# A transformer layer on eight cores: the layer norm's last step moves from VectorE to ScalarE, and the feed-forward norm is written three tiles ahead

## The reference

```python
def _layernorm(x, axis=-1, eps=1e-5):
    m = jnp.mean(x, axis=axis, keepdims=True)
    v = jnp.var(x, axis=axis, keepdims=True)
    return (x - m) / jnp.sqrt(v + eps)

x = x + attention(_layernorm(x))      # 16 heads of 128, causal, ALiBi bias, Wq Wk Wv Wo
x = x + ffn(_layernorm(x))            # below

def ffn(x):
    base = x @ W.T + b
    logits = x @ gate_w.T + gate_b
    topk_logits, topk_idx = top_k(logits, 2)
    gates = softmax(topk_logits)
    xA = einsum('nd,erd->ner', x, lora_A)
    delta = einsum('ner,eor->neo', xA, lora_B)
    return base + sum of the two chosen experts' delta * gates
```

## Time and profile before

| | us |
|---|---|
| times of two runs | 4712.88 and 4902.75 (median 4807.81) |
| the profiled execution | 4714.45, span 4712.9 on its slowest core |
| spans of the eight cores in it | 4694.5 to 4712.9 |
| PE busy | 3643.4 (77% of the span) |
| DVE busy | 1916.0 (41%) |
| ACT busy | 1149.2 (24%) |

### The profile page before, as it was taken

How to read it: one execution, slowest core, us unless ns; L and a number is a source line. 1 busy time by engine, 2 the same in 40 slices (tenths; PEclk the granted TensorE clock), 3 DMA queues, 4 the chain that set the end, 5 groups by cost and what they waited for, 6 DMA issues and landing times. The chain is left out here.

```text
span 4712.9 us, 65585 instructions; the slowest of 8 cores (4694.5 to 4712.9 us)
## 1 busy us (share of the span) xinstructions
PE 3643.4 (77%) x18452; PEld 1719.2 (36%) x18452; DVE 1916.0 (41%) x5424; ACT 1149.2 (24%) x2606; POOL 111.1 (2%) x210
## 2 busy tenths in 40 slices
PE   3588888988987694877735888888888876948777
PEld 1233434434434242333312334344344332413333
DVE  3435445455455121333334354554554551113333
ACT  3323333233233100011143232332332331000111
POOL 0000000000000001000000000000000000010000
PEclk8687787888878896888856878888888788968888
DMA  3211110110110646111131111101101106561111
GB/s 115 59 19 23 19 23 15 19 23 15 23 19 11 159 161 134 63 63 72 63 121 50 23 19 19 23 15 23 19 15 23 19 18 153 163 132 63 63 72 63
DMA packets 55537, 258.38 MB, mean 55 GB/s; under 512 B 13720, under 2 KB 13984, under 8 KB 34720
## 3 DMA queue, kind: packets, MB, share of 16 engines
q0 software_dynamic: 36464, 119.66, 13.0%
q1 hardware_dynamic: 11824, 84.20, 5.6%
q10 hardware_dynamic: 6912, 50.33, 3.0%
HBM read 273.15 MB, written 67.11 MB: 72 GB/s over the span
## 5 line engine op out<-in xcount | busy, mean ns | idle before, releaser
L852 ACT ACTIVATE prT<-dg,cstt 128x128 bf16<-128x128 f32 (+1 forms) x576 | 216.4, 386 | 1808.4 <-DVE dg L824 1328.9
L813 DVE TENSOR_SCALAR sp<-ps 128x512 f32<-128x512 f32 (+3 forms) x1104 | 631.6, 593 | 13.7 <-PE ps L806 5.4
L806 PE MATMUL ps<-QT,KT 128*128 128x512 bf16 (+3 forms) x1104 | 494.0, 489 | 184.4 <-DVE sp L813 143.6
L1118 PE MATMUL cb<-wf,cT 128*128 128x512 bf16 x2048 | 528.0, 421 | 95.3 <-DMA wf<-wf 83.6
L877 ACT ACTIVATE prT<-sp,cstt 128x128 bf16<-128x128 f32 (+2 forms) x1368 | 578.9, 488 | 16.8 <-DVE sp L813 9.8
L420 PE MATMUL bp<-wo,zTt 128*128 128x512 bf16 x2048 | 469.9, 393 | 97.1 <-DMA wo<-wo 74.1
L633 PE MATMUL pp<-xnT,wv 128*128 128x512 bf16 x2048 | 474.5, 394 | 0.0
L633 PE MATMUL pp<-xnT,wq 128*128 128x512 bf16 x2048 | 456.2, 384 | 0.0
L633 PE MATMUL pp<-xnT,wk 128*128 128x512 bf16 x2048 | 451.6, 381 | 0.0
L744 PE MATMUL pz<-va,prT 128*128 128x129 bf16 x3652 | 393.2, 266 | 26.5 <-ACT prT L877 11.4
L1118 PEld LDWEIGHTS cb<-wf,cT 128*128 128x128 bf16 x2048 | 214.6, 107 | 390.5 <-issue 205.7
(11 more groups left out here) (105 smaller groups left out, 2369.4 us busy)
## 6 DMA issues: line engine op xcount, KB each, us to landing
bx<-x SPq DMA_DIRECT2D x32, 1024.0 KB, 6.5
x2d<-b POOLq DMA_DIRECT2D x32, 1024.0 KB, 8.4
c<-x2d ACTq DMA_DIRECT2D x32, 1024.0 KB, 4.8
out<-co SPq DMA_DIRECT2D x32, 1024.0 KB, 3.9
prT<-x ACTq DMA_DIRECT2D x16, 1024.0 KB, 5.7
prT<-x SPq DMA_DIRECT2D x16, 1024.0 KB, 5.9
wv<-wv POOLq DMA_DIRECT2D x32, 512.0 KB, 6.1
wq<-wq POOLq DMA_DIRECT2D x32, 512.0 KB, 6.0
```

The costliest lines, as they stand in the source:

```text
L806: lambda e, c=c, q0=q0, n=n, bank=bank: e.matmul(psc[bank][:, 0:n], KT[:, c * 128:(c + 1) * 128], QT[:, q0 * 128: q0 * 128 + n], start=Tru ...
L813: lambda e, n=n, bank=bank, buf=buf: e.tensor_scalar(spanb[buf][:, 0:n], psc[bank][:, 0:n], 1024.0, -1024.0, ALU.min, ALU.max),
L852: soff=soff: e.activation(probsT[:, pslot:pslot + min(ncols, 128)], diagb[:, soff:soff + min(ncols, 128)] if ncols == 64 else diagb[:, 0:128],
L1118: lambda e, bi=bi, dc=dc, og=og, bk=bk: e.matmul(b["pb"][bk][:, :], b["xnT2"][bi][:, dc * 128:(dc + 1) * 128], b["wfT"][:, dc * D + og * 5 ...
```

## The change

Three things change.

1. The last step of `_plan_ln`, t8, is an ACT `activation` (Identity with scale and shift taken from two 128x1 columns) in place of DVE's `tensor_scalar`. Whoever waited for it on DVE's semaphore now waits on ACT's.
2. In the feed-forward loop, the load and the norm are no longer recorded at the head of iteration i for tile i, but at the tail of iteration i for tile i+3, behind L1174 and the store. The three tiles of the prefix serve iterations 0, 1 and 2.
3. The load's wait on `ev_out` is unchanged in text. Its place in the loop makes it mean something else: tile i+3 goes into the buffer that tile i has just left, so the load of tile i+3 waits for the last L1174 of tile i. Before, the load of tile i waited for the last L1174 of tile i-3.

```diff
@@ emit_x_load
-                    waits=[(s_dve, apply_tok[bb])])
+                    waits=[(s_act, apply_tok[bb])])
@@ emit_ln_tile
-                            w = [(s_dve, t8), (s_dve, st["ptp_copy"])]
+                            w = [(s_act, t8), (s_dve, st["ptp_copy"])]
@@ _plan_ln
-    t8 = pg.op(eng,
-               lambda e: e.tensor_scalar(xout_bf[:, :], xin[:, :],
-                                         cc[:, c0 + 6:c0 + 7],
-                                         cc[:, c0 + 7:c0 + 8],
-                                         ALU.mult, ALU.add),
-               inc=s_dve,
+    t8 = pg.op("scalar",
+               lambda e: e.activation(xout_bf[:, :], xin[:, :], AF.Identity,
+                                      bias=cc[:, c0 + 7:c0 + 8],
+                                      scale=cc[:, c0 + 6:c0 + 7]),
+               inc=s_act,
                waits=[(s_dve, t7)] + list(apply_extra))
@@ _plan_ffn
+    for t0 in range(len(prefix)):
+        apply_tok[t0 % 3] = prefix[t0][1]
     for i in range(NT):
         bi = i % 2
         bi3 = i % 3
-        if i < len(prefix):
-            ld, t_apply = prefix[i]
-        else:
-            ld = pg.op("scalar",
-                       lambda e, i=i, bi3=bi3: e.dma_start(
-                           b["x2b"][bi3][:, :], x2_d.ap()[i]),
-                       inc=sem["cxl"][bi3], amt=16,
-                       waits=[(s_dve, apply_tok[bi3]),
-                              (s_dve, ev_out[bi3]),
-                              (sem["dsb"][i % 2], b_stores[i])])
-            t_apply = _plan_ln(pg, b["x2b"][bi3], b["xnb"][bi3],
...
-        apply_tok[bi3] = t_apply
+        t_apply = apply_tok[bi3]
...
-                    w = [(s_dve, t_apply), (s_dve, ptc_copy[pk])]
+                    w = [(s_act, t_apply), (s_dve, ptc_copy[pk])]
...
+        ni = i + 3
+        if ni < NT:
+            nb3 = ni % 3
+            ld = pg.op("scalar",
+                       lambda e, ni=ni, nb3=nb3: e.dma_start(
+                           b["x2b"][nb3][:, :], x2_d.ap()[ni]),
+                       inc=sem["cxl"][nb3], amt=16,
+                       waits=[(s_act, apply_tok[nb3]),
+                              (s_dve, ev_out[nb3]),
+                              (sem["dsb"][ni % 2], b_stores[ni])])
+            apply_tok[nb3] = _plan_ln(pg, b["x2b"][nb3], b["xnb"][nb3],
+                                      b["xnb"][nb3], b["cc"], 8 * nb3, sem,
+                                      (sem["cxl"][nb3], ld),
+                                      [(s_pe, xnb_rd[nb3])], eng="vector")
```

More of the change, by code:

```diff
@@ L926, in _plan_ffn @@
         bi3 = i % 3
-        if i < len(prefix):
-            ld, t_apply = prefix[i]
-        else:
-            ld = pg.op("scalar",
-                       lambda e, i=i, bi3=bi3: e.dma_start(
-                           b["x2b"][bi3][:, :], x2_d.ap()[i]),
-                       inc=sem["cxl"][bi3], amt=16,
-                       waits=[(s_dve, apply_tok[bi3]),
-                              (s_dve, ev_out[bi3]),
-                              (sem["dsb"][i % 2], b_stores[i])])
-            t_apply = _plan_ln(pg, b["x2b"][bi3], b["xnb"][bi3],
-                               b["xnb"][bi3],
-                               b["cc"], 8 * bi3, sem, (sem["cxl"][bi3], ld),
-                               [(s_pe, xnb_rd[bi3])], eng="vector")
-        apply_tok[bi3] = t_apply
+        t_apply = apply_tok[bi3]
         trs = []
```

## The result

The changed kernel takes 4973.81 us; the ratio to the kernel before is 1.057, with a 95% interval of 1.0537 to 1.0602. It is slower, as forecast. The forecast was 4967 us in a range of 4890 to 5090. The profiled execution took 4975.72 us, its span is 4974.1 us against 4712.9 before. Single executions of every kernel here can take several per cent longer at a lower TensorE clock on one of the chip's two dies (the medians over all runs, 5220.75 and 4719.33 us, contain such ones), so the time of each kernel is the lowest of its executions without that, of which an experiment has one to three.

The account below looks back on a forecast made before the run. PE was taken to bound the kernel, with time lost where it waits for layer norms. Feed-forward +237, L600 on ACT +21 and output projection -5 us sum to +253 on 4714.45, giving 4967 us, range 4890 to 5090.

Parts of the forecast that it names:

- The load and both sums stand exposed behind the last sums: Feed-forward boundary: DVE stands at t1 while load and both ACT sums run, the next tile's copies queued behind it.
- The feed-forward term: From the end of L1174 to the large product: 17.10 against 8.56 us; with clock +9.1 us, 26 times, +237 us.
- The meeting of load and store: Feed-forward tail: load issued with the 1 MB store, 6.5 us to landing, 6.6 us from issue to first sum.
- The rival in which the load waits for all of the store: Feed-forward tail: load and store finish together, 8.8 us after the issue; 5049 us, chance 0.12.
- The clock's share: Feed-forward large product: PE's longer pause adds 0.6 us a boundary through slower clock, ends 0 and 1.2.
- L600 on ACT: First norm, serial chain: L600 takes 2.01 us on ACT against 1.35 on DVE, +0.66 us for 32 tiles, +21 us.
- The output projection, -5 us: Prefix norms ahead of L433: without L600 on DVE, PE restarts 2.7 us earlier, -5 us in two sequences.
- what an exposed norm costs: Feed-forward boundary: 4.71 + 1.21 = 5.92 us a tile, 154 us for 26 tiles.
- the rival of a hidden norm: Feed-forward: the norm comes off the path and 5.92 us return at 26 boundaries; 4576 us, chance 0.02.

Follow-up runs that it names:

- four-buffer kernel: The changed kernel with a fourth buffer c, so that the load of tile i+3 waits for the last sums of tile i-1: 4672.83 us.
- the middle place: Changed kernel with load and norm of tile i+2 between the first two and last two L1161: 4607.74 us; with L600 back on DVE 4579.73 us.

## Why the prediction was right

Right in sign, in place, and to 7 us in the time. The closeness of the number is in part luck: two terms of the feed-forward were off by some 10 us each, in opposite directions. Point by point:

- **The load and both sums stand exposed behind the last sums.** Held. DVE waits at t1 for the second sum, PE at the third transpose group, 26 times. The four-buffer kernel shows that the buffer is the cause.
- **The feed-forward term, +9.1 us a boundary, +237 us.** Measured +9.0 by the periods, +234 us. Its parts: issue 0.14 us (0.09); issue to first sum 6.8 to 7.3, in the mean 7.0 (6.6); sum to t1 4.20 (4.20); t1 to the end of t7 1.86 (1.85); to the third group 0.5 (0.67). At the boundary shown it is 13.50 us from the end of the sums to the third group, where the prediction's terms give 13.41. In the mean the stretch from the sums to the large product grew by 8.9 us, and I had taken 8.5.
- **The meeting of load and store.** I took 6.5 us to the landing from a row in which another load meets another store; it was 6.8. The rival in which the load waits for all of the store (8.8 us) is out. The Trainium skill's rule (Trainium Kernel Development and Optimization, Key Constraints: the three queues' transfers share 16 DMA engines and interleave) agrees: both transfers are slowed, 4.8 to 6.8 and 3.9 to 6.5 us, and together they take 6.8 us where one after the other they would take 8.7.
- **The clock's share, +0.6 us.** Oversized. The two halves of the large product together grew from 15.4 to 15.6 us, and the first 32 matmuls, for which I had added the 0.6, got 0.3 us shorter. So the clock took 0.2 us where I had 0.6, and this makes up for the 0.4 us by which the stretch was too short: +237 against +234 us is closer than its two terms.
- **L600 on ACT, +0.66 us a tile.** It takes 2.09 us, 0.75 more than on DVE. I had extrapolated 2.01 from passes with one column operand and named 2.11 as the end for two. The Trainium skill (ScalarE: Activation LUTs, What ACT_TABLE_LOAD costs) gives 93 ns for each 128x1 pointer operand. From 1.91 that makes 2.10 us, an estimate by that page, and the trace agrees to 10 ns. The stretch from the first transpose of the first norm to the first of the next stage grew by 13.2 and 12.1 us in the two sequences (25 us; 21 predicted); 0.75 us for 32 tiles is 24. Only the size was off.
- **The output projection, -5 us.** From the first to the last matmul of the stage it shrank by 2.7 and 3.3 us in the two sequences, as worked out.
- **The rest.** Some 8 us of the 261 us of span lie in the start and the attention stages, which the change doesn't touch; the two profiles are of different cores (4 and 0), so nothing is made of that.

One number ahead of the forecast was read too high: what an exposed norm costs. I compared a single pair of boundaries and got 5.92 us; over all of them it is 5.1, because what the first half of the product gains the second gives back. It put the rival of a hidden norm, and my expectations of the middle place, some 20 us too low. In the forecast the same pair of boundaries is where the clock's 0.6 us came from.

## What to carry to other kernels

Recording a norm further ahead does not make it earlier when its input goes into the buffer that the present tile is still reading: count the buffers against the distance, and look at what the load waits for, not at where its instruction stands. In an engine that works in order, a wait placed ahead of urgent work is paid by everything behind it, so early work belongs where the engine has an idle stretch long enough (here behind the first half of the sums), and only once its inputs have landed. Two transfers released by the same semaphore value slow each other; moving the one nobody waits for by a few microseconds gave back some 2 us each time here. And what a wait costs in clock is read from many boundaries, not from a pair.

## What the runs showed of the hardware that was not expected

Behind the same wait of 4.41 us in the same kernel, the same matmuls of 128x512 ran differently from tile to tile. The rows of PE at the two boundaries above:

```profile
1993.09 9.18 PE L1118 MATMUL cb<-wf,cT 128*128 128x512 bf16 x32
2005.93 7.07 PE L1118 MATMUL cb<-wf,cT 128*128 128x512 bf16 x32 [0.37 <-DVE co L1174]
...
2054.34 7.58 PE L1118 MATMUL cb<-wf,cT 128*128 128x512 bf16 x32
2065.74 8.68 PE L1118 MATMUL cb<-wf,cT 128*128 128x512 bf16 x32 [0.37 <-DVE co L1174]
```

9.18 and 7.07 us the one time, 7.58 and 8.68 the other: the sums, 16.25 and 16.26 us, are the same. Over 26 tiles and eight cores the two halves together took 15.2 to 15.6 us in four kernels whose stretch ahead of them is 3.4 to 17.4 us long, and 15.0 us in the one with L600 on ACT and the old order. A slow half at one boundary is therefore no sign that the wait ahead of it made it slow, and removing the wait brought no clock back. What decides which half is the slow one was not tried.
